# Zero matmuls in TensorE's waits of a routing stage, up to the first expert block

## The reference, cut to what matters

```
logits = jnp.einsum('bsd,de->bse', xn, Wr) + br
top_vals, top_idx = jax.lax.top_k(logits, K)              # K = 2 of E = 8
w = jax.nn.softmax(top_vals, axis=-1)
for e in range(E):
    h = jax.nn.gelu(jnp.einsum('bsd,dh->bsh', xn, W1[e]) + b1[e], approximate=False)
    y_e = jnp.einsum('bsh,hd->bsd', h, W2[e]) + b2[e]
    y = y + y_e * w_full[..., e, None]
```

## Time and profile before

| what | value |
|---|---|
| median of 3 runs | 466.09 us (465.48, 466.09, 471.38) |
| profiled execution, its own time | 465.14 us |
| its span | 463.3 us |
| TensorE clock, mean over the span | 0.891 |
| TensorE busy (matmul) | 380.6 us, 82% |
| VectorE busy | 289.0 us, 62% |
| ScalarE busy | 221.3 us, 48% |
| GpSimd busy | 144.9 us, 31% |

### The profile page before, as it was taken

One profiled execution on the slowest core, in us unless ns is written; L12 is line 12 of the kernel. 1 busy time (PEld: TensorE's weight loads), 2 busy tenths in 40 slices (PEclk: granted clock), 3 DMA queues, 4 the chain that ended last, 5 costly groups with the idle time before them and its releaser, 6 DMA issues.

```text
span 463.3 us, 12828 instructions
## 1 busy us (share of the span) xinstructions
PE 380.6 (82%) x4362; PEld 343.1 (74%) x4363; DVE 289.0 (62%) x642; ACT 221.3 (48%) x351; POOL 144.9 (31%) x253
## 2 busy tenths in 40 slices
PE   6884889999995889860469999999999999999300
PEld 2773889999995566750369999999999999999200
DVE  5959988999947544658934444444444444444773
ACT  3585677888881365640044444444444444443000
POOL 3363000000000500000065665566665666553200
PEclk9995799999999878955569999999999999999755
DMA  8710799999999999210022221222222221224899
GB/s 208 176 36 1 167 178 224 214 212 215 219 221 126 267 363 384 82 55 1 1 69 70 69 69 68 71 75 68 69 68 79 68 68 68 68 69 115 231 241 312
DMA packets 112698, 62.17 MB, mean 134 GB/s; under 512 B 86625, under 2 KB 106743, under 8 KB 112544
## 3 DMA queue, kind: packets, MB, share of 16 engines
q1 hardware_dynamic: 102244, 42.95, 38.3%
q0 software_dynamic: 6272, 14.93, 9.9%
q10 hardware_dynamic: 4156, 3.96, 2.6%
HBM read 27.70 MB, written 13.64 MB: 89 GB/s over the span
## 4 chain that ended last, share of the span: by engine, by line
PE 66%; DMA 9%; DVE 8%; ACT 5%; issue 4%; SPq 3%; POOL 2%; ACTq 1%; DVEq 0%; POOLq 0%
PE psum L974 20%; PE psum L985 19%; PE psum L845 9%; PE psum L836 7%; PE psum L893 3%; PE psum L915 3%; PE psum L963 3%; DMA w_sb<-pair_rows 2%; DMA at<-cts 2%; SPq L384 2%; DMA edge_key_lo<-kl_f 2%; DMA next_i<-in_dst_dram 1%; POOL gath L462 1%; ACT cts L625 1%; DMA pair_rows<-yb,scol 1%
## 5 line engine op out<-in xcount | busy, mean ns | idle before, releaser
L974 PE MATMUL psum<-xgT,w_now 128*128 128x128 f32 x832 | 102.9, 277 | 0.0
L974 PEld LDWEIGHTS psum<-xgT,w_now 128*128 128x128 f32 x832 | 98.5, 194 | 0.2
L985 PE MATMUL psum<-w_sb,hT 128*128 x416 | 98.4, 380 | 0.0
L625 ACT CAST cts<-psum 128x1000 bf16<-128x1000 f32 x100 | 78.3, 815 | 22.9 <-PE psum L836 22.4
L985 PEld LDWEIGHTS psum<-w_sb,hT 128*128 128x128 f32 x416 | 75.1, 190 | 8.4 <-issue 0.3
L713 ACT ACTIVATE hT<-up 128x512 f32<-128x512 f32 x52 | 32.7, 630 | 99.1 <-DVE up L1382 99.1
L845 PE MATMUL psum<-z,at 125*128 (+1 forms) x1875 | 70.6, 194 | 5.4 <-DMA at<-cts 5.4
L702 ACT COPY w_now<-w_sb 128x1024 f32 x52 | 54.4, 1046 | 33.1 <-DVEq L1347 22.0
L845 PEld LDWEIGHTS psum<-z,at 125*128 125x128 bf16 x1875 | 65.2, 99 | 6.5 <-DMA at<-cts 4.6
L504 POOL DMA_INDIRECT pair_rows<-yb,scol x52 | 51.6, 993 | 46.5 <-issue 33.3
L1382 DVE TENSOR_TENSOR up<-psum,b1T 128x512 f32<-128x512 f32 x52 | 36.0, 692 | 48.1 <-PE psum L974 48.1
(11 more groups left out here) (230 smaller groups left out, 352.3 us busy)
## 6 DMA issues: line engine op xcount, KB each, us to landing
w_sb<-in_L_ffn_W_dram SPq DMA_DIRECT2D x2, 4096.0 KB, 23.9
res<-in_x_dram SPq DMA_DIRECT2D x5, 560.0 KB
token_rows<-tok SPq DMA_DIRECT2D x5, 560.0 KB
tok<-pair_rows SPq DMA_DIRECT2D x5, 560.0 KB
w_sb<-pair_rows SPq DMA_DIRECT2D x5, 560.0 KB
out_dram<-res ACTq DMA_DIRECT2D x5, 560.0 KB
b_sb<-in_L_ffn_b_dram SPq DMA_DIRECT2D x1, 1024.0 KB, 25.2
xg<-token_rows,gcol POOLq DMA_INDIRECT x52, 2.7
```

Source lines behind the costliest of these rows:

```text
L625: act.copy(cts[:, par, :, d0:d0 + nw * WD].rearrange("p h (b d) -> p b h d", b=nb), psum[:, bank:bank + nb, 0:wb * WC].rearrange("p b (d h ...
L974: last = pe.matmul(psum[:, j % 2, c * P:(c + 1) * P], w1_now[:, j % 2, k, c * P:(c + 1) * P], xgT[:, j % 2, k, :], start=(k == 0), stop=(k ...
L985: last = pe.matmul(psum[:, 4 + j % 2, 0:D], hT[:, j % 2, k, :], w2_sb[:, ds(e, 1), k, :].rearrange("p a h -> p (a h)"), start=(k == 0), st ...
```

## The change

Four calls of `keep_awake` are added to TensorE's stream: 16 zero matmuls into bank 5 before the wait for `sel`, 12 into bank 7 behind the two counting matmuls, 6 into bank 7 behind the matmuls of k = 0, and 24 into bank 7 behind those of k = 1. That makes 58 zero matmuls with their weight loads. No wait, no semaphore and no other engine's stream is changed, and nothing reads what they write.

```diff
+            keep_awake(16, 5)
             pe.wait_ge(r_dve, 2)
             selv = sel[:].rearrange("p t e -> p (t e)")
             pe.matmul(psum[0:T, 4, 0:NT * NX], later[0:T, 0:T], selv, start=True, stop=True)
             pe.matmul(psum[:, 5, 0:NT * NX], ones16[0:T, :], selv, start=True, stop=True).then_inc(r_pe, 1)
+            keep_awake(12, 7)
 
             pe.matmul(psum[:, 6, 0:2 * NB], ones16[0:1, :], zeros16[0:1, 0:2 * NB], start=True, stop=True)
             for k in range(2):
                 pe.wait_ge(pair_oh, k + 1)
                 for t in range(NT):
                     last = pe.matmul(...)
                 last.then_inc(pair_mm, 1)
-
+                keep_awake(6 if k == 0 else 24, 7)
 
             pe.wait_ge(L["experts"], 48)
             pe.wait_ge(slots_ready, 1)
```

## The result

| what | before | changed |
|---|---|---|
| median | 465.78 us (4 executions) | 471.01 us (4 executions) |
| ratio, 95% interval | 1 | 1.0136 [1.0075, 1.0197] |
| profiled execution, its own time | 465.14 us | 471.73 us |
| its span | 463.3 us | 469.9 us |
| TensorE clock, mean | 0.891 | 0.892 |

The changed kernel is slower, by 1.36% in the first measurement, and its median lies above the predicted range of 464.4 to 469.3 us.

A forecast was written before the change was run, and what follows sets the result against it. VectorE was taken to bound the routing stage and TensorE the expert blocks. First filler +1.2 - 0.2, second and third 0, fourth -0.4 gave +0.6 us on 465.6, so 466.2 us, range 464.4 to 469.3.

The forecast's parts named there:

- The bounds of the kernel: VectorE sets the routing stage; TensorE sets the expert blocks, so their start moves the end microsecond for microsecond.
- the second hand-over: VectorE's read of bank 6 after L949 in the routing stage: TensorE and VectorE level within 0.1 us.
- The first filler: 16 before the wait for `sel`: 5.1 us in a 3.9 us wait, so VectorE resumes 1.0 us late.
- The deduction of 0.2 us for the faster counting: Counting matmuls after `sel`, 0.70 us before, estimated 0.2 us shorter at the fast clock.
- My bound of 2.7 us: Upper end of the delay from the 16 before `sel`, if the clock doesn't rise: 6.6 - 3.9 us.
- the overshoot: Rival, 20 in 100: the 16 outlast the wait for `sel` and delay L942; +2.7 to +3.5 us, 468.3 to 469.1.
- The second and third filler: 12 behind the counting and 6 between L949's groups, inside VectorE's waits: 0 us each, the 6 up to +0.8.
- The +0.8 us that the overshoot rival adds: The 6 between L949's groups, if all slow: 2.5 us in a 1.74 us gap, pushing the second group back.
- The fourth: 24 before the first block: 5.2 us fast in a 7.06 us wait, ending too early; gain 0.4 us.
- its prize: First block at the high clock, transposes and L974 in 2.0 us instead of 3.94: 1.9 us, mostly expected lost.
- The sum: +1.2 - 0.2 + 0 + 0 - 0.4 = +0.6 us over the whole kernel.
- The base: 465.6 us for the unchanged kernel, the middle of the profiled execution and the median of three runs.

The follow-up runs named there:

- e1: The changed kernel run again with no edit: median 472.19 us against 466.87 for the unchanged kernel, ratio 1.0122.
- e2: Changed kernel with only the 16 before the wait for `sel`, the 12, 6 and 24 left out: 468.09 us against 466.87 unchanged, ratio 1.0107.
- e10: The changed kernel run a third time with no edit: median 469.63 us against 467.0 for the unchanged kernel, ratio 1.0060.
- e9: Changed kernel with only the first filler, doubled from 16 to 32, later calls left out: 474.13 us against 467.0 unchanged, ratio 1.0138.
- e6: Changed kernel with only the 24 before the first block, the 16, 12 and 6 left out: 465.51 us against 468.1 unchanged, ratio 0.9939.
- e11: Only the 24 before the first block, the same file measured a second time: 466.05 us against 467.0 unchanged, ratio 0.9989.
- e3: Changed kernel without the 16; the 12, 6 and 24 stay: 469.01 us against 466.87 unchanged, ratio 1.0077.
- e8: Changed kernel without the 16, the same file measured a second time: 467.07 us against 468.1 unchanged, ratio 0.9991.

## Why the prediction was wrong

**The bounds of the kernel** were read rightly: VectorE sets the routing stage, the second hand-over is level, and the first block's start goes through the expert blocks: from the transposes of the sixth block to those of the last it is 171.8 us in all fourteen traces.

**The first filler** is the term that was mis-sized. I took 8 of the 16 at the low clock, with a rise after 3.4 us, and a delay of 1.2 - 0.2 = 1.0 us. The rise came after 5.7 us in the changed kernel, hence 13 of them and part of the next at the low clock, and the delay was 2.07 us; e1 gave 2.08, e2 (a rise after 5.3 us) 1.87. Only e10 was near it: a rise after 3.9 us, 1.13 us. The deduction of 0.2 us for the faster counting was right: from the start of the counting to `tot` it is 0.45 us against 0.70. The rises of 3.0 to 3.9 us that I had from the earlier trace rows are rightly read, but four rises of one execution didn't bound the next one. My bound of 2.7 us held (at 0.43 us a piece, the price at the low clock, it would be 2.9, and 6.8 us of fillers in a wait of 3.9 give 2.9 too, not my 3.0), and the overshoot, which I had as a rival with 20 in 100 from a rise later than 3.4 us on, is what happened in three of the four traces that have sixteen fillers there. The Trainium skill (TensorE: Matmul & The Clock Gate, The HAM clock gate) says that the count before the rise differs between runs of one kernel, 6, 11 or 14; by that rule 14 at the low clock were possible, and these traces agree: 9 in e10, 11 in e9, 12 in e2 and 13 in the changed kernel and e1. The delays that I had worked out from it for 11 and 14, 1.9 and 2.5 us, were nearer to three of the four measured ones than my own 1.0.

**The second and third filler** delay nothing, as forecast: 17.81 us from `tot` to `slot`, against 17.82. The step holds with all six fillers at the low clock too (2.77 us); the second group ended at 233.3, still before VectorE's 233.75. Its speed-up, 2.52 to 1.54 us, is hidden as forecast. The +0.8 us that the overshoot rival adds for six fillers at the low clock didn't come, because the group behind them became fast.

**The fourth** lost its prize, for the reason given: 24 fast fillers end too early. Of 1.9 us I counted on 0.4. The three traces have 0.07, 0.01 and 0.39 us, from 3.70, 3.76 and 3.38 against 3.77; since the copy of before has 3.55, even the 0.39 is hardly a gain. e6 and e11 support the reason: with 1.5 us less between the last filler and the rows, 1.7 us come back. What I had not seen is that the change defeats itself here: the 6, with the two groups of L951 around them, raise the clock ahead of the 24 (at about 232.1 us in the changed kernel) and so shorten them. The 12 have no part in it there: after them the clock fell at about 221.8, before the first group.

**The sum** was +0.6 us; by the traces of the changed kernel it is 36.22, 36.19 and 34.85 against 34.13, so +2.1, +2.1 and +0.7 us up to the third L965. That alone would have been 467.7 us, inside the range.

**The end of the kernel** is a term that I put at nothing: "cost only where counted". From the last group's first logit to the end of the span the unchanged kernel took 257.6 and 256.3 us, and the changed one 260.4, 259.9 and 259.3, which is 2.9 us more on average. Of these, 1.8 lie before the third L965 and 1.1 behind the last expert block, nearly all in the landing of the last write of rows (6.92, 6.35 and 6.78 us against 5.85 and 5.49). The expert blocks between are the same.

**The base** is the other half of the miss. The forecast stood on three executions and one trace. The unchanged kernel, its copy included, ran 103 times in all, between 460.19 and 479.56 us with a median of 467.28, 1.7 above my 465.6, and its MLP stage took 55.94 us in one trace and 59.09 in the other. My range allowed 0.3 us for this. The first four executions of the changed kernel (median 471.01) and its first trace, with 3.8 us lost before the first filler, held bad luck on top of the cost; the third measurement had 1.0060. The miss of 4.8 us (471.01 against 466.2) is then 1.7 of base, 2.3 of cost (2.9 against 0.6) and 0.8 of luck, the first median against the 470.22 of all executions.

**What stays open.** Over its 22 executions the changed kernel's median is 470.22 us, 2.9 above the 467.28 of the unchanged one (1.9 to 5.2 by resampling), and the ratios say 0.6 to 1.4%, or 3 to 6 us. The traces show 0.7 to 2.1 us in the stretch that the change touches, and with the last stage 2.9 on average. That the last stage's part belongs to the change is not shown: seven traces against seven speak for it, and no run sets it apart. e3 and e8, the later fillers without the sixteen, gave 1.0077 and 0.9991, too far apart to settle it. That the length of the MLP stage goes with the clock granted in it is read from traces; no run was made that sets it.

## What to carry to other kernels

A filler in an in-order queue is free only up to the end of the wait, priced at the low clock and with the latest rise: 16 in a wait that holds 9 cost 1.1 to 2.1 us each time. In these traces fillers won only where they reached up to the work that they were for; 24 ending 0.8 us before it brought 1.7 us, the same 24 made faster by other fillers ahead of them ended 2.3 us before it and brought nothing. Where an unchanged copy's ratio is 1.005 and one file gives 1.008 and 0.999, judge an effect of 1 or 2 us by the same stretch in several traces, and get the spread of the unchanged kernel before setting a range. Follow such a stretch to the end of the kernel, too: a mark at the third block's transposes missed 0.3 to 0.9 us in e3 and e8 and about 1 us in the last stage.

## What the runs showed that I had not expected

The clock rose 3.9, 4.7, 5.3 and 5.7 us after the first filler began, for the same instruction after the same work (e10, e9, e2, changed). It outlived a gap of 2.29 us without work and four transposes, to fall 3.8 us after the last filler (changed). And the MLP stage, which lies ahead of all that was changed, takes 54 to 59 us from one execution to the next.
